# The feed-forward of a perceiver block with GELU kept in its bank, rows normalized on ScalarE, and weight sums made by four-column products

## What is computed

```
x = x + cross_attention(layernorm(x), ctx, mask)    # 4 heads of 128, one KV head, RMS norm, rope
x = x + causal_attention(layernorm(x))              # 16 heads of 32, over 64 tokens of a batch item
x = x + ffn(layernorm(x))

def ffn(x):                                         # W_fc (2048, 512), W_proj (512, 2048)
    h = gelu(x @ ternary(W_fc).T)                   # exact gelu
    h = (h - mean(h)) * rsqrt(var(h) + 1e-5) * ln_w + ln_b      # over 2048
    return h @ ternary(W_proj).T
ternary(W) = sign(W) * min(round(|W| / (mean|W| + 1e-6)), 1)    # -1, 0 or 1
```

## Time and profile before

| what | value |
|---|---|
| median of 3 runs | 1143.78 us (1143.51 to 1144.44) |
| profiled execution, its own time | 1138.14 us |
| its span from first to last instruction | 1136.3 us |
| mean granted TensorE clock | 0.964 of full speed |
| TensorE / VectorE / ScalarE / GpSimd busy | 83% / 67% / 45% / 34% |

### The profile page before, as it was taken

How to read it: one execution, slowest core, us unless ns; L and a number is a source line. 1 busy time by engine, 2 the same in 40 slices (tenths; PEclk the granted TensorE clock), 3 DMA queues, 4 the chain that set the end, 5 groups by cost and what they waited for, 6 DMA issues and landing times. The chain is left out here.

```text
span 1136.3 us, 22651 instructions
## 1 busy us (share of the span) xinstructions
PE 944.9 (83%) x7278; PEld 793.8 (70%) x7278; DVE 758.7 (67%) x1340; ACT 506.5 (45%) x1044; POOL 390.1 (34%) x500
## 2 busy tenths in 40 slices
PE   0898878888788988789699988888788888979994
PEld 0787767776676766569588877777566666868873
DVE  3587767666666767662664656666669967687775
ACT  2565445654455554543332333343464444534551
POOL 1344444444444444410110112111133353354533
PEclk9999999999999999989699999999899999999997
DMA  5532223222223223313444434434212002020011
GB/s 166 158 86 53 75 85 110 72 60 76 81 81 91 71 72 108 108 39 85 140 131 124 131 105 118 122 88 131 54 47 75 1 29 83 1 102 1 19 56 41
DMA packets 100609, 93.02 MB, mean 82 GB/s; under 512 B 45729, under 2 KB 62194, under 8 KB 100466
## 3 DMA queue, kind: packets, MB, share of 16 engines
q1 hardware_dynamic: 99856, 91.11, 27.7%
q10 hardware_dynamic: 578, 0.13, 0.1%
q0 software_dynamic: 32, 0.02, 0.0%
HBM read 74.37 MB, written 12.66 MB: 77 GB/s over the span
## 5 line engine op out<-in xcount | busy, mean ns | idle before, releaser
L244 PE MATMUL bank<-f,f 128*128 128x512 f32 (+3 forms) x5032 | 646.8, 304 | 65.7 <-issue 26.1
L244 PEld LDWEIGHTS bank<-f,f 128*128 128x128 f32 (+2 forms) x5032 | 507.3, 171 | 153.9 <-issue 69.1
L219 PE MATMUL bank<-f,f 128*128 128x128 f32 x896 | 134.7, 283 | 74.7 <-DVE f L619 29.0
L233 DVE TENSOR_TENSOR f<-bank,f 128x512 fp32r<-128x512 f32 x227 | 151.3, 683 | 55.3 <-ACT f L230 53.3
L230 ACT ACTIVATE f<-bank 128x512 fp32r<-128x512 f32 x227 | 130.3, 592 | 113.9 <-PE bank L219 108.7
L219 PEld LDWEIGHTS bank<-f,f 128*128 128x128 f32 x896 | 104.5, 145 | 96.4 <-DVE f L619 30.1
L1205 PE MATMUL bank<-f,f 128*128 128x512 f32 x512 | 130.0, 397 | 0.4 <-DVE f L1171 0.4
L1184 POOL TENSOR_TENSOR f<-f,f 128x512 f32<-128x512 f32 x60 | 83.4, 1390 | 133.4 <-ACT f L1182 132.6
L1205 PEld LDWEIGHTS bank<-f,f 128*128 128x128 f32 x512 | 97.3, 191 | 23.2 <-issue 2.0
L934 POOL TENSOR_TENSOR f<-f,f 128x512 f32<-128x512 f32 x32 | 33.4, 1043 | 209.3 <-DVE f L931 209.3
L468 POOL TENSOR_TENSOR f<-f,f 128x512 f32<-128x512 f32 x32 | 41.9, 1310 | 158.9 <-ACTq L74 136.0
(11 more groups left out here) (110 smaller groups left out, 1014.7 us busy)
## 6 DMA issues: line engine op xcount, KB each, us to landing
f<-in_ctx_dram SPq DMA_DIRECT2D x71, 256.0 KB, 2.8
f<-x_scratch SPq DMA_DIRECT2D x64, 256.0 KB, 3.5
f<-in_x_dram SPq DMA_DIRECT2D x32, 256.0 KB, 3.0
x_scratch<-f SPq DMA_DIRECT2D x32, 256.0 KB, 2.0
f<-in_L_ffn_W_fc_dram SPq DMA_DIRECT2D x32, 256.0 KB, 2.9
f<-in_L_ffn_W_proj_dram SPq DMA_DIRECT2D x32, 256.0 KB, 3.4
f<-in_ktab_dram SPq DMA_DIRECT2D x71, 64.0 KB, 1.9
f<-f SPq DMA_DIRECT2D x64, 64.0 KB, 2.4
```

Source lines behind the costliest of these rows:

```text
L219: f = lambda e, i=i, a=a: e.transpose(dst[:, i, :], a, ident[0:rows, 0:rows])
L233: return maybe("dve", lambda e: e.tensor_tensor(lo, src, hi.bitcast(F32), ALU.subtract), sem(name + "_lo"), waits, when)
L244: f = lambda e, i=i, a=a, b=b: e.matmul(dst, a, b, start=(first and i == 0), stop=(last and i == n - 1), skip_group_check=check)
```

## The change

The feed-forward's GELU is written back into its bank. The high part, the square, the low part and the running sum read it there, VectorE's two after ScalarE's three, and only then is the bank free; the buffers `g3` go. For the first block of a group the sum is a copy. Rows of the third stage are normalized on ScalarE (`s3_apply`): a small VectorE instruction makes minus mean times root, ScalarE applies scale and bias; this and the statistics stand earlier in their slots. The weight sums are made by TensorE: `s3_rows` puts high and low parts of `ln_w` and `ln_b` side by side as four columns, sixteen products with the blocks of P gather four rows in one bank, which is held from slot `H0 + 6` to `H0 + 13`, and `s3_wrow` adds high and low row and spreads them with a selecting matrix. `s3_base` stands four slots earlier for groups 1 to 3. In the attention stage the absolute sums take 26 slots' pace, the quantization one slot each, and `w_T(n)` stands one slot after `w_quant(n)`.

```diff
--- before.py
+++ after.py
@@ -1093,14 +1093,14 @@
     at(B2 + 3, 8.7, s2_outs)
     at(B2 + 3, 8.8, lambda: s2_wload(3))
     for n in range(64):
-        s = B2 - 2 + (n * (4 * ni - 6)) // 64
+        s = B2 - 2 + (n * (4 * ni - 38) // 32 if n < 32 else 4 * ni - 70 + n)
         if n < 4:
             at(B2 - 1, 0.5, lambda n=n: w_load(n))
         if n < 32:
             at(s + 3, 0.3, lambda n=n: w_abs(n))
         else:
             at(s + 3, 0.3, lambda n=n: w_quant(n))
-            at(s + 3, 4.5, lambda n=n: w_T(n))
+            at(s + 4, 4.5, lambda n=n: w_T(n))
     B3 = B2 + 4 * ni
 
 
@@ -1113,10 +1113,9 @@
     r = [Region(CONST + 8192 * ((nb - 2 - n) % NG), CONST + 8192 * ((nb - 2 - n) % NG + 1)) for n in range(NG)]
     Gh, Gl = r[0](3, D, dt=F32R), r[1](3, D, dt=F32R)
     sq3 = r[0](D), r[1](D)
-    sums, wsum = r[2](2, D), r[2](2, D)
+    sums, wsum, lwb, sel = r[2](2, D), r[2](D), r[2](NF, 4, dt=F32R), r[2](2, 128)
     outs.at = CONST + EARLY + LATE + 16384
     XFh, XFl = [late(4, D, dt=F32R)], [outs(4, D, dt=F32R)]
-    g3 = late(3, D)
     smu, svar, srs, snm, ssq = late(4), late(4), late(4), late(4), late(4)
     r = Region(CONST + EARLY, CONST + EARLY + LATE)
     Po, acc = r(4, D), r(2, 2, D)
@@ -1145,6 +1144,13 @@
             tok["WP", n] = op("act", lambda e: e.activation(dst, src, ACT.Copy), sem("f_W"), w)
         else:
             tok["WP", n] = op("dve", lambda e: e.tensor_copy(dst, src), sem("f_WF0"), w)
+
+    def s3_apply(i):
+        u = i % 2
+        tb = op("dve", lambda e: e.scalar_tensor_tensor(rs2[:, u, 1:2], mv2[:, u, 0:1], -1.0, rs2[:, u, 0:1],
+                                                        ALU.mult, ALU.mult), sem("f_dv"), [tok["rs", i]])
+        tok["xn", i] = [op("act", lambda e: e.activation(xn[:, u, :], xa[:, u, :], ACT.Identity, bias=rs2[:, u, 1:2],
+                                                         scale=rs2[:, u, 0:1]), sem("f_gelu"), [tb, *d2("xnT", i - 2)])]
 
     def s3_T(i):
         g, j = i // 4, i % 4
@@ -1163,37 +1169,32 @@
         rows = [t for j in range(4) for t in tok["XT", ni + 4 * g + j]]
         tk = products(bank[k][:, :], terms, "f_h", [tok["WF", f // 4], *rows, *gfree[k]])
         tok["h", q] = [tk]
-        tg = op("act", lambda e: e.activation(g3[:, y, :], bank[k][:, :], ACT.Gelu), sem("f_gelu"),
-                [tk, *d2("gread", q - 3)])
-        give(k, [tg])
-        th = op("act", lambda e: e.activation(Gh[:, y, :], g3[:, y, :], ACT.Copy, scale=lwp[:, f:f + 1]),
+        gp = bank[k][:, :]
+        tg = op("act", lambda e: e.activation(gp, gp, ACT.Gelu), sem("f_gelu"), [tk])
+        th = op("act", lambda e: e.activation(Gh[:, y, :], gp, ACT.Copy, scale=lwp[:, f:f + 1]),
                 sem("f_G_hi"), [tg, tok["lwb"], *tok["sc", ni - 1], *d2("p", q - 3)])
-        tl = op("dve", lambda e: e.scalar_tensor_tensor(
-            Gl[:, y, :], g3[:, y, :], lwp[:, f:f + 1], Gh[:, y, :].bitcast(F32), ALU.mult, ALU.subtract),
-            sem("f_G_lo"), [th, tok["lwb"], *tok["sc", ni - 1], *d2("p", q - 3)])
-        tok["G", q] = [th, tl]
-        v = g % 2
+        v, z = g % 2, q % 2
         if f == 0:
-            ts = op("act", lambda e: e.activation(acc[:, v, 1, :], g3[:, y, :], ACT.Square), sem("f_gelu"),
+            ts = op("act", lambda e: e.activation(acc[:, v, 1, :], gp, ACT.Square), sem("f_gelu"),
                     [tg, *wfree[63], *d2("stat", g - 2)])
             tok["acc2", g] = [ts]
         else:
-            z = q % 2
-            ts = op("act", lambda e: e.activation(sq3[z][:, :], g3[:, y, :], ACT.Square), sem("f_gelu"),
+            ts = op("act", lambda e: e.activation(sq3[z][:, :], gp, ACT.Square), sem("f_gelu"),
                     [tg, *tok["sc", ni - 1], *tok.get(("sqr", z), [])])
             tp = op("pool", lambda e: e.tensor_tensor(acc[:, v, 1, :], acc[:, v, 1, :], sq3[z][:, :], ALU.add),
                     sem("f_acc2"), [ts, *tok["acc2", g]])
             tok["acc2", g] = tok["sqr", z] = [tp]
-        if f:
-            a = g3[:, (q - 1) % 3, :] if f == 1 else acc[:, v, 0, :]
-            ta = op("dve", lambda e: e.tensor_tensor(acc[:, v, 0, :], a, g3[:, y, :], ALU.add), sem("f_dv"),
-                    [tg, tl, *tok.get(("acc", g), []), *wfree[63], *d2("stat", g - 2)])
-            tok["acc", g] = [ta]
-            tok["gread", q] = [ta, ts]
-            if f == 1:
-                tok["gread", q - 1] = [ta, tok["sq0"], th]
+        tl = op("dve", lambda e: e.scalar_tensor_tensor(
+            Gl[:, y, :], gp, lwp[:, f:f + 1], Gh[:, y, :].bitcast(F32), ALU.mult, ALU.subtract),
+            sem("f_G_lo"), [th, ts, tok["lwb"], *tok["sc", ni - 1], *d2("p", q - 3)])
+        tok["G", q] = [th, tl]
+        if f == 0:
+            ta = op("dve", lambda e: e.tensor_copy(acc[:, v, 0, :], gp), sem("f_dv"), [ts, th, *wfree[63], *d2("stat", g - 2)])
         else:
-            tok["sq0"] = ts
+            ta = op("dve", lambda e: e.tensor_tensor(acc[:, v, 0, :], gp, acc[:, v, 0, :], ALU.add), sem("f_dv"),
+                    [ts, th, *tok["acc", g]])
+        tok["acc", g] = [ta]
+        give(k, [tl, ta])
 
     def s3_p(q):
         g, f = q // NF, q % NF
@@ -1241,22 +1242,34 @@
         t5 = D_(lambda e: e.scalar_tensor_tensor(snm[:, :], smu[:, :], -1.0, srs[:, :], ALU.mult, ALU.mult), [t4])
         tok["nm3", g] = [t4, t5]
 
+    def s3_rows():
+        for z, src in enumerate((lwp, lbp)):
+            th = op("act", lambda e, z=z, src=src: e.activation(lwb[:, :, z], src[:, :], ACT.Copy), sem("f_gelu"),
+                    [tok["lwb"], *tok["pv", ni - 1]])
+            tl = op("dve", lambda e, z=z, src=src: e.tensor_tensor(
+                lwb[:, :, 2 + z], src[:, :], lwb[:, :, z].bitcast(F32), ALU.subtract), sem("f_dv"),
+                [th, tok["lwb"], *tok["pv", ni - 1]])
+            ts = op("dve", lambda e, z=z: e.tensor_tensor(
+                sel[0:4, z, :], ident[0:4, z:z + 1].to_broadcast([4, 128]),
+                ident[0:4, 2 + z:3 + z].to_broadcast([4, 128]), ALU.add), sem("f_dv"), [t_id, *tok["pv", ni - 1]])
+        tok["rows"] = [th, tl, ts]
+
     def s3_wsum(f):
-        src = WP[:, f, :].bitcast(F32)
-        for z, (eng, s) in enumerate((("dve", lwp), ("dve", lbp))):
-            w = [tok["WP", f // 4], tok["lwb"], *tok["pv", ni - 1], *tok.get(("wsum", z), [])]
-            if f == 0:
-                fn = lambda e, z=z, s=s: e.tensor_scalar(wsum[:, z, :], src, s[:, f:f + 1], None, ALU.mult)
-            else:
-                fn = lambda e, z=z, s=s: e.scalar_tensor_tensor(wsum[:, z, :], src, s[:, f:f + 1], wsum[:, z, :],
-                                                                ALU.mult, ALU.add)
-            tok["wsum", z] = [op(eng, fn, sem("f_dv"), w)]
+        if f == 0:
+            tok["kw"] = take()
+        k = tok["kw"]
+        tk = op("pe", lambda e: e.matmul(bank[k][0:4, :], lwb[:, f, :], WP[:, f, :], start=f == 0, stop=f == NF - 1),
+                sem("f_p"), [tok["WP", f // 4], *tok["rows"], *(gfree[k] if f == 0 else ())])
+        if f == NF - 1:
+            tok["wsum"] = op("act", lambda e: e.activation(wsum[0:4, :], bank[k][0:4, :], ACT.Copy), sem("f_gelu"),
+                             [tk, *tok["pv", ni - 1]])
+            give(k, [tok["wsum"]])
 
     def s3_wrow():
         for z in range(2):
             k = take()
-            tk = op("pe", lambda e, z=z, k=k: e.matmul(bank[k][:, :], ones[:, :], wsum[:, z, :], start=True, stop=True),
-                    sem("f_p"), [*tok["wsum", z], t_on, *gfree[k]])
+            tk = op("pe", lambda e, z=z, k=k: e.matmul(bank[k][:, :], sel[0:4, z, :], wsum[0:4, :], start=True, stop=True),
+                    sem("f_p"), [tok["wsum"], *tok["rows"], *gfree[k]])
             ts = op("act", lambda e, z=z, k=k: e.activation(sums[:, z, :], bank[k][:, :], ACT.Copy), sem("f_gelu"),
                     [tk, *tok["pv", ni - 1]])
             give(k, [ts])
@@ -1292,19 +1305,20 @@
         g, j = i // 4, i % 4
         s = H0 + 16 * (g - 1) + 3 + 3 * j if g else H0 - 9 + 2 * j
         at(s - 3, 0, lambda i=i: ln_load(ni + i))
-        at(s - 2, 5, lambda i=i: ln_stats(ni + i))
-        at(s - 1, 5, lambda i=i: ln_apply(ni + i))
+        at(s - 2, 1.55, lambda i=i: ln_stats(ni + i))
+        at(s - 1, 1.55, lambda i=i: s3_apply(ni + i))
         at(s, 5.2, lambda i=i: s3_T(i))
         at(H0 + 16 * g + 9 + j, 0, lambda i=i: s3_res(i))
-        at(H0 + 16 * g + 17 + (j if g < ng - 1 else 0), 4, lambda i=i: s3_base(i))
+        at(H0 + 16 * g + (13 if g else 17) + j, 4, lambda i=i: s3_base(i))
         at(H0 + 16 * g + 18 + (j if g < ng - 1 else 0), 4 + j / 8, lambda i=i: s3_fin(i))
     for q in range(NF * ng):
         at(H0 + q, 1.5, lambda q=q: s3_h(q))
         at(H0 + q + 2, 2.5, lambda q=q: s3_p(q))
     for g in range(ng):
         at(H0 + 16 * g + 16 + 1, 2.2, lambda g=g: s3_stat(g))
+    at(H0 + 4, 4.5, s3_rows)
     for f in range(NF):
-        at(H0 + 4 + f * 3 // 4, 4.5, lambda f=f: s3_wsum(f))
```

(1 more changed line is left out.)

## The result

The changed kernel takes 1090.47 us (median of 4 runs, 1088.71 to 1093.12) against 1143.97 for the kernel before, also a median of 4; the ratio is 0.9534, with a 95% interval of 0.9514 to 0.9554. That is 53.5 us, 4.7%, faster.

A forecast was written before the change was run, and what follows sets the result against it. TensorE was taken to bound the kernel, with holes where it waits for late VectorE. Terms 16 + 7.4 + 14.7 - 2.6 + 2.1 = 37.6 us, off 1143.78, gave 1106.2 us; range 1093 to 1124.6.

The forecast's parts named there:

- the price of the attention stage: Attention with quantization: of 21.3 us of TensorE waits for the quantization, 16 us gained, bounds 5 and 21.3.
- the same difference gives: Final sum: the median lies 5.64 us above the profiled execution, and this offset was kept for the changed kernel.
- the changes of group: Feed-forward: 6.7 us gained at each of two with new rows, 3.0 excess left; 1.3 at the last; together 14.7.
- the first group: Feed-forward, GELU 5 to 17: of 12.0 us excess, 3.6 goes to products and 1.0 stays; gain 7.4 us.
- the tail: End of the kernel: small product and sums run faster without GpSimd's residual additions beside them; gain 2.1 us.
- the first slots: Start of the feed-forward: the new apply delays ScalarE's copy of the last exponentials; loss 2.6 us, bounds 0 and 4.
- Rival (a): Attention stage: the stall only moves to what is late next, 3 of 21.3 us gained; time 1119, chance 0.19.
- rival (d): Attention stage: VectorE's quantization waits for earlier transposes on two buffers, lengthening each of 32 slots; time 1163, chance 0.07.
- my sign for it (below 5 us): Attention stage: line 1031's waits on VectorE for the transposes were to stay below 5 us.
- the s3_fin pair: Changes of group: two VectorE passes with two SBUF inputs beside GpSimd, priced at 1.7 to 2.7 us together.
- rival (b): Feed-forward: reading the bank does not speed line 1171 and the sum; gain 25 us, time 1119, chance 0.06.
- Rival (c): Feed-forward: ScalarE's apply needs two table loads of 1.283 us at each of 12 applies; time 1125, chance 0.04.

The follow-up runs named there:

- same: The kernel before, unchanged, run once more with a profile: 1143.07 us, ratio 0.9996.
- bank_apply: The kernel before with GELU kept in its bank and third-stage rows normalized on ScalarE, all else as before: 1119.14 us, ratio 0.9793.
- no_apply: The changed kernel with third-stage rows normalized on VectorE again, statistics and normalization late in their slots: 1094.96 us, ratio 0.9578 to the kernel before.

## Why the prediction fell short

**The step that failed** is the price of the attention stage, "Of the 21.3 us I take 16 as gained", with 21.3 as the best case of the range. It counts waits alone and takes TensorE's own work as fixed. In a usual execution of before (the run `same`) the stage takes 183.61 us, TensorE busy for 155.56; in the changed kernel 159.96, busy for 148.31 with as many matmuls. So the stage gives 23.6 us: 16.4 of idle time, which is what was priced, and 7.2 of work that runs shorter at a granted clock of 0.99 in place of 0.94. The new slots do this by themselves: with them alone the stage takes 159.83 us at 0.98.

The same step was hidden once more in the sum: "the median of the three runs lies 5.64 higher, and the same difference gives". That difference is not an offset which every kernel has. 4.4 us of it are the clock of this stage, of which the profiled execution of before lost less than usual (0.97), and the new slots remove it. That this profile was a fast one was bad luck; the mistake was not to ask what the 5.64 us were. In numbers: the forecast is 15.9 us short; 7.6 are this stage, 4.7 the changes of group, 1.6 the first group and 0.8 the tail, the first slots take 0.3 away, and 1.5 lie outside these stretches. The two changes of group with new rows also hold some 2 us each of work that became shorter (TensorE busy for 26.8 and 27.1 us at 0.95 before, 24.9 and 25.0 at 1.00 after), but their price was taken against rows at full clock and had it in.

Of the 8.5 us between profiled and usual executions, the clock explains those 4.4. Most of the rest may be the first stage in the profile of the changed kernel: 547.48 us to M0, where the thirteen other profiles have 542.15 to 546.22. There is no second profile of that kernel, so this is not shown.

**The sum, term by term.** In the attention stage 5.3 us were left for what is late next, and about that much was: idle time fell by 16.4 us, not by 21.3. At the end of the stage the changed kernel waits for 3.9 us, where before waited 6.4 for line 1034; two low parts of line 233, behind masks and statistics on VectorE, end 0.1 us ahead of it:

```profile
793.64 4.46 PE L244 MATMUL bank<-f,f 128*128 128x512 f32 x12 [3.89 <-issue]
```

Rival (a), which left 3 of 21.3, is out. The wait of rival (d) came, and my sign for it (below 5 us) failed; VectorE's waits at 500 to 809 us in the changed kernel, against 2.7 us in the earlier trace rows:

```profile
DVE f L1031 <- PE bank L1046: 19.4, 7, 4.0
```

TensorE did not pay for it: its wait for the exponentials behind the masks (line 938) is 5.6 us in three times before and after. The case of (d), every slot longer, did not occur.

The first group gave 9.0 for 7.4. The products cost 4.2 us (slots of 4.15 us for 3.63, two products in each; forecast 3.6), only 0.35 us of excess was left, and s3_wrow fell from 3.52 to 1.98 us. Its f32 products have four rows to sum now, but that is not why. The timeline of bank_apply, where they have 128:

```profile
907.26 1.98 PE L1259 MATMUL bank<-f,f 128*128 128x512 f32 x4 [0.35 <-DVE f L1252]
```

The earlier trace rows was a row at low clock, behind 2.5 us in which TensorE was idle. The stretch around it in the kernel before:

```profile
906.19:910.69 4.50, 3.04 (x5) 1.48 (x5) 2.68 (x4) 1.47 (x3) 0.00 (x0) 0.63 0.00 0
```

I had put 1.5 us of low clock into the clean work.

Each of the two changes of group with new rows was priced at 3.0 us left over, and 1.4 and 0.5 were; at the last, 0.6 was priced and nothing was left. I had priced the s3_fin pair at 1.7 to 2.7 us; in the groups by line it takes 872 and 752 ns in the mean, 1.62, below my lower end. VectorE's own prices were right, 750 and 680 ns for 751 and 681, so rival (b) is out. The Trainium skill ("SBUF — State Buffer", Who interferes with whom) says that a VectorE instruction contends with a GpSimd one that reads SBUF when it has two SBUF inputs. The traces agree in both directions: with one SBUF input the sum takes 680 ns beside GpSimd, and with two it takes 709 ns once GpSimd is quiet.

The first slots lost 2.9 (2.6 forecast), by the step that was named: the last P V products wait 5.91 us for 3.43. Taking the apply back gives only 1.6 of it (no_apply), as the products behind the shorter wait then take 5.64 us for 5.09, and the next eight 2.61 for 2.00. The tail gave 2.9 for 2.1, as the four additions of GpSimd no longer stand beside it. Line 1242, line 1241 before, takes 0.16 us for 1.23:

```profile
1078.43 0.16 DVE L1242 SCALAR_TENSOR_TENSOR f<-f,f 128x4 f32<-128x4 f32 x1 [1.42 <-POOL f L263]
```

Rival (c) is out: no table load stands at any of the 16 applies. That agrees with the Trainium skill ("ScalarE: Activation LUTs", Table sets: the hidden batching unit), which has identity in every set.

The prediction also did not see that its edits do not add up. At a change of group the bank alone gives 2.3 and 0.7 us, the apply alone 0.9 and 1.7, both 8.3 and 8.1. In the first group the weight sums off VectorE give 9.0, bank and apply 10.1, all three 9.0.

## What to carry to other kernels

A stall can cost more than its own length. Where the granted clock is low behind a stall, removing the stall can return slow work too: here 16.4 us of waiting and 7.2 of work. So read the granted clock beside each wait and each row that serves as a price, and cut the profiled execution and one more into the same stretches before adding a forecast to a median. When one engine is late for several reasons at once, judge the edits together: each alone may look worthless or harmful, as the apply did, and one of them may be superfluous, as the weight sums on TensorE were.

## What the runs showed of the hardware

A GELU from a bank into the same bank takes 582 ns, 598 into SBUF; the scaled copy reads a bank in 688 ns and SBUF in 724. Scale and bias by row from SBUF to SBUF take 815 ns, 91 more than I had priced. A VectorE instruction on 128x4 with two SBUF inputs took 1.23 us when GpSimd had just begun a 128x512 addition and 0.16 without, so a tiny instruction too can lose a microsecond. The sum of line 1189 takes 0.69 us at the shortest and 1.61 in the median, and its mean of 1330 ns is a mixture of the two.
